# Keys and V' halves gathered apart for four tiles instead of two, and the adjacency loaded in 4 KB runs, in a sparse graph-attention kernel

## The reference

```
q = x @ Wq.T + bq;  k = key @ Wk.T + bk;  v = value @ Wv.T + bv
s = (q @ k.T) / 64 * adj
s = where(abs(s) < 1e-5, -1e9, s)
y = softmax(s, axis=-1) @ v @ Wm.T + bm
out = layernorm(x + y)
```

## Time and profile before

| | |
|---|---|
| median of 3 runs (lowest to highest) | 562.37 us (561.5 to 562.74) |
| the profiled execution: its time, its span | 560.05 us, 558.2 us |
| PE busy | 510.8 us, 92% |
| DVE busy | 337.4 us, 60% |
| ACT busy | 229.7 us, 41% |
| POOL busy | 232.0 us, 42% |
| DMA | 160.81 MB, mean 288 GB/s |
| chain that ended last, by engine | PE 43%, DMA 22%, DVE 19%, SP's queue 8%, ACT 4% |

### The profile page before, as it was taken

The page is one execution under the profiler, slowest core; times in us unless marked ns, Lnnn a source line. Parts: engine busy times, 40 slices in busy tenths (PEclk is TensorE's granted clock), DMA queues, the critical chain, the costliest instruction groups (busy, mean ns, idle before and its releaser), DMA issues.

```text
span 558.2 us, 5679 instructions
## 1 busy us (share of the span) xinstructions
PE 510.8 (92%) x1678; PEld 267.3 (48%) x1678; DVE 337.4 (60%) x756; ACT 229.7 (41%) x463; POOL 232.0 (42%) x205
## 2 busy tenths in 40 slices
PE   6999999999389974999999989999999999999983
PEld 3444444444134443556555545555555555555651
DVE  1574678976961047678688888765645543453552
ACT  0233123333123222334552554464373464465473
POOL 3000020008600366466675565655664565466400
PEclk9999999999879996999999999999999999999996
DMA  9999999999999999595899899656547455346422
GB/s 350 423 406 426 426 422 387 384 397 418 408 395 356 340 418 389 175 360 206 320 383 408 318 292 354 217 162 212 164 150 242 105 182 187 99 144 227 114 76 79
DMA packets 43957, 160.81 MB, mean 288 GB/s; under 512 B 9874, under 2 KB 9874, under 8 KB 37778
## 3 DMA queue, kind: packets, MB, share of 16 engines
q1 hardware_dynamic: 20690, 102.21, 47.0%
q0 software_dynamic: 16992, 38.26, 22.3%
q10 hardware_dynamic: 6240, 19.92, 9.0%
HBM read 161.98 MB, written 25.17 MB: 335 GB/s over the span
## 4 chain that ended last, share of the span: by engine, by line
PE 43%; DMA 22%; DVE 19%; SPq 8%; ACT 4%; issue 3%; POOL 0%; ACTq 0%; DVEq 0%; POOLq 0%
DMA big<-adj_tiles 16%; PE bank L496 13%; PE bank L602 11%; PE bank L622 10%; SPq L353 7%; DVE big L898 7%; PE bank L578 5%; DMA table<-key 4%; DMA kv<-table,index 2%; PE bank L612 1%; DVE big L933 1%; DVE slots L931 1%; PE bank L593 1%; DVE big L901 1%; DVE score L1035 1%
## 5 line engine op out<-in xcount | busy, mean ns | idle before, releaser
L392 POOL DMA_INDIRECT kv<-table,index x90 | 100.1, 1112 | 111.5 <-PE bank L622 89.2
L487 PE MATMUL bank<-kv,big 128*128 128x512 f32 x256 | 113.6, 604 | 10.6 <-DMA big<-valueT 10.6
L496 PE MATMUL bank<-big,M 128*128 128x512 f32 x256 | 120.0, 596 | 0.0
L421 POOL DMA_INDIRECT adj_g<-adj_cols,index x96 | 107.8, 1123 | 29.3 <-issue 29.3
L898 DVE TENSOR_TENSOR big<-big 128x2048 bf16<-128x2048 f32 x32 | 73.2, 2288 | 41.3 <-DMA big<-adj_tiles 41.3
L602 PE MATMUL bank<-keyT,qT 128*128 128x384 f32 x256 | 88.9, 490 | 6.2 <-issue 4.9
L622 PE MATMUL bank<-kv,probT 128*128 128x512 f32 x192 | 89.7, 604 | 0.9 <-ACT probT L809 0.6
L487 PEld LDWEIGHTS bank<-kv,big 128*128 128x128 f32 x256 | 49.1, 193 | 72.6 <-issue 61.0
L602 PEld LDWEIGHTS bank<-keyT,qT 128*128 128x128 f32 x256 | 47.6, 190 | 46.7 <-issue 19.1
L496 PEld LDWEIGHTS bank<-big,M 128*128 128x128 f32 x256 | 44.6, 192 | 34.2 <-issue 34.2
L1030 DVE SCALAR_TENSOR_TENSOR score<-bank,c_cols,adjT 128x384 f32<-128x384 f32 x32 | 19.8, 618 | 67.8 <-PE bank L602 66.4
(11 more groups left out here) (99 smaller groups left out, 522.4 us busy)
## 6 DMA issues: line engine op xcount, KB each, us to landing
big<-adj_tiles SPq DMA_DIRECT2D x32, 2048.0 KB, 11.3
big<-valueT ACTq DMA_DIRECT2D x8, 1024.0 KB, 13.4
x_buf<-x SPq DMA_DIRECT2D x32, 256.0 KB, 4.5
table<-key SPq DMA_DIRECT2D x8, 1024.0 KB, 22.8
out<-y_buf SPq DMA_DIRECT2D x32, 256.0 KB, 3.7
big<-xT SPq DMA_DIRECT2D x6, 1024.0 KB, 12.0
table<-qT ACTq DMA_DIRECT2D x4, 1024.0 KB, 20.9
table<-y_buf ACTq DMA_DIRECT2D x4, 1024.0 KB, 28.5
```

The lines of the kernel that those rows point to most:

```text
L392: pool.indirect_dma_start(kv[:, b, c, :], None, table, bass.IndirectOffsetOnAxis(index[:, t, c:c + 1], 0), bounds_check=N - 1, oob_is_err= ...
L421: pool.indirect_dma_start(adj_g[:, b, c, :], None, adj_cols, bass.IndirectOffsetOnAxis(index[:, t, CH + c:CH + c + 1], 0),).then_inc(adj_g ...
L487: mm = nc.tensor.matmul(bank[4 + t % 2][:, :], col_buf[nb % 2][:, d, k * P:(k + 1) * P], G[:, d, :], start=(d == 0), stop=(d == DC - 1))
L496: mm = nc.tensor.matmul(ps[:, :], M[:, d, a * P:(a + 1) * P], col_buf[nb % 2][:, d, :], start=(d == 0), stop=(d == DC - 1))
```

## The change

- `EARLY` is 4: tiles 0 to 3 get keys from `key` and V' halves from `table` in separate gathers. The full gathers begin with tile 4.
- G moves from `kv` to the first four output buffers, so `kv` is zeroed in two pieces and the late third one is gone. V' has three buffers instead of four; the waits on their stores follow.
- The adjacency lies in DRAM as four pieces per tile. In each, a partition has a run of 1024 elements (4 KB), where it had one of 4096 (16 KB). The SBUF side and the number of bytes are as before.

```
-VS = 4
+VS = 3
-EARLY = 2
+EARLY = 4
+PIECES = 4
...
-        G, w_left, w_right = (kv_flat[:, kv_half + i * 2048:kv_half + (i + 1) * 2048].rearrange("p (e d) -> p e d", e=DC)
-                              for i in range(3))
+        w_left, w_right = (kv_flat[:, kv_half + i * 2048:kv_half + (i + 1) * 2048].rearrange("p (e d) -> p e d", e=DC)
+                           for i in range(2))
...
-        v_out = [qT[:, 1, :, :], y_buf[:, 0:DC, :], y_buf[:, DC:2 * DC, :], qT[:, 0, :, :]]
+        v_out = [qT[:, 1, :, :], y_buf[:, DC:2 * DC, :], qT[:, 0, :, :]]
+        G = y_buf[:, 0:DC, :]
...
-        V_SLOT = (0, 1, 2, 3, 0, 1, 2, 0)
+        V_SLOT = (0, 1, 2, 0, 1, 2, 0, 1)
...
-                sp.dma_start(adj_buf[t % 2], adj_tiles[t]).then_inc(adj_in[t % 2], 16)
+                sp.dma_start(adj_buf[t % 2].rearrange("p (j n) -> p j n", j=PIECES), adj_tiles[t].rearrange("j p n -> p j n")
+                             ).then_inc(adj_in[t % 2], 16)
...
-            nc.gpsimd.memset(kv_flat[:, kv_half + 2048:2 * kv_half], 0.0).then_inc(kv_zeroed, 1)
+            nc.gpsimd.memset(kv_flat[:, kv_half:2 * kv_half], 0.0).then_inc(kv_zeroed, 1)
...
             for t in range(EARLY):
                 gather_keys(t)
                 gather_adj(t)
-            for t in range(EARLY, KV):
-                gather_adj(t)
...
             for t in range(EARLY):
                 gather_values(t)
-            nc.gpsimd.memset(kv_flat[:, kv_half:kv_half + 2048], 0.0).then_inc(kv_zeroed, 1)
-            pool.wait_ge(kv_zeroed, 3)
             pool.wait_ge(table_in, 16 * NB)
...
-                    act.wait_ge(v_stored[V_SLOT[3] if u == 0 else V_SLOT[0]], 16 * V_USES[V_SLOT[3] if u == 0 else V_SLOT[0]])
+                    act.wait_ge(v_stored[2 if u == 0 else 0], 16 * V_USES[2 if u == 0 else 0])
...
-                if t == 0:
-                    for k in (1, 2):
-                        dve.wait_ge(v_stored[k], 16 * V_USES[k])
+                if t == DC:
+                    dve.wait_ge(v_stored[1], 16 * V_USES[1])
...
-        "adj_tiles": np.ascontiguousarray(a.transpose(1, 3, 0, 2, 4)).reshape(T, P, N),
+        "adj_tiles": np.ascontiguousarray(
+            a.transpose(1, 3, 0, 2, 4).reshape(T, P, PIECES, N // PIECES).transpose(0, 2, 1, 3)),
```

## The result

The changed kernel takes 574.85 us (median of 4 runs, 570.93 to 576.63), the kernel before 561.93 us (559.07 to 562.74): a ratio of 1.023 with an interval of 1.016 to 1.030, so slower by 2.3%. The forecast was 568.8 us.

A forecast was written before the change was run, and what follows sets the result against it. The prediction took full DMA queues up to tile 20's landing as the bound: 11.5 us later less 5.1 us gained, +6.4 us on 560.05, gives 566.5, and 568.8 us with the median 2.3 us higher; range 557 to 575.5.

The forecast's parts named there:

- The sum: Whole kernel: tile 20 landing 11.5 us later, less 5.1 us gained, makes +6.4 us.
- What the removed wait is worth: At tile 2, PE's 8.32 us wait for the key gather goes; 5.1 us gained if tile 20 lands as before.
- L + 15.9: Start of second stage: tile 2's scores are softened 15.9 us after adjacency tile 20 lands, the time called L.
- (a): Ahead of tile 20: key and V' gathers of two more early tiles, 2.1 MB, delay it 5.4 us (5.0 to 8.6).
- (c): Just before tile 20 lands: the first full gather competes with its load, adding 0.8 us (0 to 1.5).
- (b): Adjacency tiles 0 to 20: 4 KB runs cost 0.25 us a tile, 5.3 us in all (0 to 8.4).
- What costs nothing: First stage: PE's 10.60 us valueT wait goes uncredited; later DVE tiles, second list and V' buffers fit within slack.
- The signs named ahead: Profile after: waits gone or moved, tile 20 some 11 us later, DVE idle over 10 us, DMA share still 1.0.
- The wait comes out whole: Rival, first stage: the DMA has room, tile 20 lands no later, 5.1 us gained, 557.3 us; chance 0.30.
- The low ends: Rival, ahead of tile 20: runs almost free, its landing moves 4 to 6 us, 562.4 us; chance 0.10.
- The distance of 512 KB: Rival, adjacency loads: a partition's runs lie 512 KB apart, halving the rate, some 660 us; chance 0.03.
- Late elsewhere: Rival: lateness elsewhere, above all adjacency tiles 22 to 31 against DVE, more than 13 us in all; chance 0.05.

The follow-up runs named there:

- The experiment on the slot list: The changed kernel with PE taking its part of the first slot list after V' row block 20 instead of 17: 568.61 us, ratio 1.0127.

## Why the prediction was right in its sign and short in its size

The kernel is slower for the reason that stood there, a tile 20 that lands later than the removed wait is worth. The sum was +6.4 us; measured are +12.9 by the ratio and +16.6 in the profiled executions.

**What the removed wait is worth: held.** L + 15.9 was the step; 15.94 after and 15.93 with the early tiles alone. 22.8 - 5.1 = 17.7 us is what tile 2's softening moved by, so the waits behind L are the ones that were named.

**(a), the gathers: held; (c), the first full gather: there was none.** Up to L the kernel after moved 5.37 MB on q0, 0.79 of it adjacency columns, so 4.58 MB for four tiles and 2.3 for two, where 2.1 was forecast. At the 394 GB/s of the early tiles alone up to L that is 5.8 us. For (c) 0.8 us was added, but in the changed kernel the first full gather is tile 4's, and it waits for the V' product of tile 0. It is issued behind L: at 216.29 us with the early tiles alone (L 213.59), and after (L 228.82) here:
```profile
233.89 0.99 POOL L395 DMA_INDIRECT kv<-table,index  x1 [19.19 <-PE bank L621]
```
So its cost ahead of L is nothing. The sum of the two, 6.2 us, is near the 7.5 measured with the early tiles alone, in part by luck; 1.7 of the 7.5 are not placed. These parts alone would have been +1.1 us by the forecast and +0.4 us by the ratio.

**(b), the 4 KB runs: the term that was mis-sized.** 5.3 us forecast, with 8.4 as the upper end; the runs move L by 228.82 - 213.59 = 15.2 us. The experiment on the slot list splits that in two: 7.5 us are left with the later list (221.04 against 213.59), and 7.8 go with the halt. The 7.5, read as slower transfer, lie inside the bounds. In the first 105 us q1 took 3.51 us a MB (105 / 29.93) instead of 3.18 (105 / 33.00), 0.68 us a tile where 0.25 was forecast. By the shares of the queue rows above, q1's own transfers took 2.63 us a MB (0.749 x 105 / 29.93) instead of 2.45 (0.769 x 105 / 33.00), 0.38 us a tile; the rest is time of the engines that q1 no longer had. Of the 3.07 MB that q1 is behind at 105 us only 0.06 went to q10. Some of the delay is made up later: tile 11 is 12.0 us late against the early tiles alone (104.69 against 92.68), tile 20 with the later list 7.5. At 141 us q1 of that kernel is 3.49 MB behind the early tiles alone, but q10 is 1.61 MB ahead, so that later less of q10 is left to move beside the adjacency and the key copies. The Trainium skill's price (DMA: Bandwidth & Descriptors, "Why small descriptors are slow (HBM only)"), from which 1.7% a tile was worked out, is near the rows beside stores: from 60 to 66 us 417 GB/s after and 426 before, 2.1%, though the kernels with 16 KB runs scatter from 413 to 433 there. It is far short of 40 to 84 us, 389 against 425, where the measurement decides.

**"What costs nothing" failed.** The other 7.8 us are a wait that the prediction did not look for. It read the slack of the second list (8 us) but not of the first: there PE is at L516 at 108.64 and DVE had the list at 106.7, 2 us. It had tile 17 move by 9 us; tile 11 moved by 14.6 and tile 17 by 25.4 (163.49 against 138.09), PE stopped for 12.07 us, and the DMA engines ran dry, which the sum had excluded by taking the share of 1.01 over into the changed kernel. It is 0.97 there, 0.83 from 84 to 125 us. The slack of the second list didn't hold either: with the first halt gone PE waits 5.24 us there. PE entered the second stage at 212.0 us, measured at its first L577, and not at 190 to 195. That is the late tile 19 more than the halt: its end was forecast at 171 and came at 190.8, L559 waits for it, and with the later list PE still enters at 208.28.

**The signs named ahead.** The valueT wait goes, the wait at L559 comes, there is no gather wait at tile 2, GB/s is lower in the adjacency's stretch: all seen. Tile 20 some 11 us later: it was 22.8. DVE idle for it by more than 10 us: seen with the early tiles alone (11.96), not after (3.10), since PE's late entry has DVE late too; 3 us more of that and tile 20 would not have mattered. DMA share still 1.0: wrong.

**The rivals.** The wait comes out whole: no; it pays only with tile 20 moved up as well (ratio 0.9948), or tiles 20 and 21 (0.9868), not by itself (1.0007). The low ends, L moving by 4 to 6 us: no, the early tiles alone are above that. The distance of 512 KB: no (391 against 389 GB/s). Late elsewhere by more than 13 us, adjacency tiles 22 to 31 above all: the lateness was elsewhere, but ahead of L, not behind it.

## What to carry to other kernels

When a load in a full DMA stage gets slower, go through every place in the stage where one engine takes another's result in a fixed order, and read the slack of each; the smallest counts (here 2 us), and a halt there costs DMA time if the halted engine also feeds the queues (here 5.8 us by the ratios). A wait removed at the end of such a stage is worth only what the transfer that ends next allows: move that transfer up with it, since here early tiles alone and the order alone gave nothing, and both together 0.5%, or 1.3% with tile 21 moved up too. Before a term is added for a transfer that competes with the last one, see what releases it in the changed kernel: here the first full gather came behind tile 20. A price for a run length taken from one queue's mean did not hold for the mix here, where the run length also changed how soon the other queue was served.

## What the runs showed of the hardware

- Adjacency loads with little or nothing beside them (74 to 82 us, single looks) ran at 390 to 434 GB/s in 16 KB runs and at 341 to 381 in 4 KB runs.
- The run length of one queue changed how soon another was served: V' stores landed after 29.8 us (median) beside 16 KB runs and after 16.5 us beside 4 KB runs.
- PE's clock was granted at 1.00 up to its halt at 109 us and at 0.50, 1.2 GHz, from 121 to 125 us, when it worked again: six small matmuls of L515 took 1.42 us instead of 0.80.
